# Recommender tower kernel: three or four one-hot chunks of each half stand ahead of the gram fills

## The reference, cut to what matters

```python
e = stack([tbl_t[ids[:, t]] for t in range(26)], axis=1)       # (2048, 26, 128)
combined = concatenate([dense[:, None, :], e], axis=1)          # (2048, 27, 128)
G = einsum('bfd,bgd->bfg', combined, combined)                  # one gram matrix for each sample
z = concatenate([dense, G[:, iu, ju], dense], axis=1)           # upper triangle, 607 columns
h = maximum(z @ W_top1 + b_top1, 0)                             # 512
h = maximum(h @ W_top2 + b_top2, 0)                             # 256
y = h @ W_top3                                                  # (2048, 1)
```

## Time and profile before

| | |
|---|---|
| median of 3 runs | 543.87 us |
| profiled execution | 548.43 us |
| its span | 546.6 us |
| TensorE busy | 418.0 us, 76% |
| VectorE busy | 275.6 us, 50% |
| GpSimd busy | 243.9 us, 45% |
| ScalarE busy | 142.9 us, 26% |
| mean granted TensorE clock | 0.881 of full speed |

### The profile page before, as it was taken

The page is one execution under the profiler, slowest core; times in us unless marked ns, Lnnn a source line. Parts: engine busy times, 40 slices in busy tenths (PEclk is TensorE's granted clock), DMA queues, the critical chain, the costliest instruction groups (busy, mean ns, idle before and its releaser), DMA issues.

```text
span 546.6 us, 10182 instructions
## 1 busy us (share of the span) xinstructions
PE 418.0 (76%) x4392; PEld 385.7 (71%) x4392; DVE 275.6 (50%) x365; ACT 142.9 (26%) x355; POOL 243.9 (45%) x264
## 2 busy tenths in 40 slices
PE   2477765759878596985969768794887949778998
PEld 2466664759776595975959768693886849767987
DVE  4389853854445454444454545445552465434322
ACT  4355121522122111222112222122221222112432
POOL 6726373553626355262553616446163552616100
PEclk9869995978889798787988879799787989979999
DMA  7954631221212112121221211222020311211000
GB/s 201 259 141 105 200 85 33 83 62 38 66 42 79 49 49 69 40 74 44 54 62 50 72 36 58 58 65 71 27 86 28 83 43 38 80 31 38 22 11 1
DMA packets 19775, 37.38 MB, mean 68 GB/s; under 512 B 5930, under 2 KB 8626, under 8 KB 19732
## 3 DMA queue, kind: packets, MB, share of 16 engines
q0 software_dynamic: 8192, 16.79, 11.5%
q1 hardware_dynamic: 5492, 9.85, 6.8%
q10 hardware_dynamic: 6048, 10.10, 6.0%
HBM read 36.71 MB, written 0.01 MB: 67 GB/s over the span
## 4 chain that ended last, share of the span: by engine, by line
PE 56%; another core or an unknown queue 19%; issue 10%; ACT 7%; DVE 5%; DMA 2%; SPq 1%; DVEq 0%; ACTq 0%
PE psB L431 19%; PE psG L457 14%; PE psB L506 7%; PE psB L415 6%; PE psB L513 6%; PE psB L500 3%; DVE one_hot L730 3%; ACT ET L633 2%; DMA ET<-tbl 2%; ACT ET L653 2%; PE psB L468 1%; DVE tab_lo L741 1%; ACT Zp L672 1%; ACT psG L605 1%
## 5 line engine op out<-in xcount | busy, mean ns | idle before, releaser
L354 POOL DMA_INDIRECT E<-tbl,gidx x256 | 243.0, 949 | 264.2 <-PE psB L415 163.5
L730 DVE TENSOR_TENSOR one_hot<-oidx,psR 125x1024 fp32r<-125x1024 int32 (+1 forms) x176 | 200.8, 1169 | 172.0 <-remote 130.7
L431 PE MATMUL psB<-one_hot,tab_hi 125*128 125x256 f32 x672 | 126.1, 308 | 24.4 <-issue 11.7
L457 PE MATMUL psG<-ET 128*52 128x52 f32 x2048 | 87.5, 259 | 70.8 <-issue 38.7
L457 PEld LDWEIGHTS psG<-ET 128*52 128x52 f32 x2048 | 79.2, 172 | 79.5 <-issue 45.6
L431 PE MATMUL psB<-one_hot,tab_lo 125*128 125x256 f32 x672 | 118.7, 296 | 14.4 <-issue 11.3
L431 PEld LDWEIGHTS psB<-one_hot,tab_hi 125*128 125x128 f32 x672 | 99.4, 202 | 31.7 <-issue 26.5
L431 PEld LDWEIGHTS psB<-one_hot,tab_lo 125*128 125x128 f32 x672 | 99.0, 201 | 16.7 <-issue 12.7
L633 ACT COPY ET<-psB 128x512 f32<-128x512 f32 x64 | 40.8, 638 | 89.2 <-PE psB L415 58.1
L777 DVE COPY_PREDICATED S<-second,psG 116x208 f32<-116x208 int32 x64 | 25.0, 391 | 50.1 <-ACT S L662 49.6
L662 ACT COPY S<-psG 116x208 f32<-116x208 f32 x64 | 21.3, 332 | 100.8 <-PE psG L457 95.3
(11 more groups left out here) (55 smaller groups left out, 217.3 us busy)
## 6 DMA issues: line engine op xcount, KB each, us to landing
oidx<-hot_idx ACTq DMA_DIRECT2D x35, 256.0 KB
E<-tbl,gidx POOLq DMA_INDIRECT x256
ET<-tbl SPq DMA_DIRECT2D x3, 448.0 KB
oidx<-hot_idx SPq DMA_DIRECT2D x5, 256.0 KB
dense<-dense_pairs SPq DMA_DIRECT2D x8, 128.0 KB
ZH<-tbl SPq DMA_DIRECT2D x2, 448.0 KB
S<-tbl SPq DMA_DIRECT2D x2, 448.0 KB
Zd<-dense_rows ACTq DMA_DIRECT2D x7, 128.0 KB, 2.0
```

The costliest lines, as they stand in the source:

```text
L354: nc.gpsimd.indirect_dma_start(E[:, n % SLOTS, i, :], None, gathered[feature_and_tile(n, i)[0]], bass.IndirectOffsetOnAxis(ap=gidx[:, 4 * ...
L431: product = nc.tensor.matmul(bank[:, t % 2 * DUO:(t % 2 + 1) * DUO], tab[0:ROWS_P, TABLE_BASE[t] + k0 + i, :], one_hot[0:ROWS_P, m % RING, ...
L457: gram = nc.tensor.matmul(psG[g % 2][q * LANE:q * LANE + M, a * M:(a + 1) * M], two[:, 0:M], two[:, PAIR:], start=True, stop=True)
L730: nc.vector.tensor_tensor(one_hot[0:ROWS_P, m % RING, 0:many], ids, rows, ALU.is_equal).then_inc(hot_full[m % RING], 1)
```

## The change

In every half that has chunks, the first of them go ahead of the gram fills: chunks 0, 1 and 2 in odd halves (`FILL_LAST[0]` is 3), chunks 11 to 14 in even ones. The rest are spread as before, among fewer steps. In half 2 the W1 steps belong to chunks 11 to 15, so four of the five go ahead of the gram fills with their chunks.

```diff
-        left = hots
+
+        ahead = FILL_LAST[0] if late else 4
+        first, left = hots[:ahead], hots[ahead:]
         if late:
             after = spread(left, parts(d - 1)[:M1]) if d else left
...
-        return grams + spread(turns, with_W1(after) if h == 2 else after)
+        if h == 2:
+            first, after = with_W1(first), with_W1(after)
+        return first + grams + spread(turns, after)
```

## The result

The changed kernel took 549.12 us (547.72 to 550.45, 4 runs) against 543.83 us beside it: ratio 1.0103, 95% interval 1.0079 to 1.0128. It is slower by 1.0%; the forecast was 533.4 us, faster by 1.9%. Its profiled execution took 550.45 us, with a span of 548.6. The profiled execution of the kernel before has a span of 546.6 and took 4.6 us more than that kernel's median, the changed kernel's only 1.3 more, so the two traces differ by 2.0 us where the medians differ by 5.3. Ratios here are taken over undisturbed executions alone, so they can differ a little from the quotient of two medians.

The account below looks back on a forecast made before the run. TensorE's completions, held back beside GpSimd's gathers, were taken as the bound. Even halves gaining 2.3 us and odd ones losing 0.8, times 7, gave 10.5 us off the 543.87 us median: 533.4 us, range 518 to 560.

Parts of the forecast that it names:

- C: Rival: even halves keep two runs of eight gathers, VectorE's builds delay gram copies; 22 us slower, 566; chance 0.18.
- D: Rival: even halves run sixteen gathers in one stretch; 24 us slower, 568, or 556 in one pair of two; chance 0.18.
- Point 4: Even halves' gathers: twelve plus four, release 17.1 us after the first gather instead of 23.4; 2.3 us gained.
- Points 1 and 2: Odd halves: moved chunks fill TensorE's idle, 2.9 to 1.0 us gained; builds ahead of VectorE's gram copy, 1.7 us lost.
- Point 5: Odd halves' gathers: two runs of eight remain, next first gather at 33.8 us against 33.0; 0.8 us lost.
- points 2 and 3: Builds ahead of VectorE's gram copy in odd halves, 1.7 us lost; even halves' early chunks and queue, 0.5 us lost.

Follow-up runs that it names:

- f1_change: The changed kernel itself, unaltered, measured again beside the kernel before (548.49 us): 549.15 us, ratio 0.9988.
- f2_from2: The change from half 2 on, half 1 keeping the order of the kernel before: 545.03 us, ratio 0.9933 to the kernel before.
- f4_from3: The change from half 3 on, halves 1 and 2 keeping the order of before, measured again: 546.73 us, ratio 0.9975 to the kernel before.
- e6_mid: The change in halves 3 to 13 only, VectorE's queue as in the change: 546.26 us, ratio 0.9948 to the kernel before.
- e4_queue: The whole change, but VectorE walks each half's four gram copies before the moved chunks' builds: 542.19 us, ratio 0.9963 to the kernel before.
- e5_mid_queue: The change in halves 3 to 13 only, with VectorE's gram copies ahead of the moved builds: 532.74 us, ratio 0.9806 to the kernel before.
- e1_odd: The change in odd halves only, even halves keeping the order of the kernel before: 552.43 us, ratio 1.0184 to the kernel before.
- e12_from3_queue: The change from half 3 on, including half 14, with VectorE's gram copies ahead of the moved builds: 536.17 us, ratio 0.9749 to the kernel before.
- e3_from3: The change from half 3 on, halves 1 and 2 keeping the order of before, first measurement: 545.91 us, ratio 1.0057 to the kernel before.

## Why the prediction was wrong

**Right.** What bounds the kernel: completions of TensorE held back beside GpSimd's gathers. The runs made that firmer than the trace could (549.7 to 401.6 us). The measured 549.1 us lies in the stated range of 518 to 560 only by the partial forms of C and D, not by the forecast. Point 4: even halves went to twelve and four gathers, release 17.0 us after the first (said: 17.1), next first gather 31.7 us after it (said: 32.0). Points 1 and 2: gram fills at 256.6, 22.3 us after the first gather (said: 20.6), with a wait of 1.46 us for VectorE (said: 1.7 in odd halves).

**Point 5 was wrong in its mechanism.** It kept two runs of eight in odd halves; they became twelve and four as well, and the distance is 32.4 us, not 33.8. The third transpose was let out early enough, or just after the eighth gather (`f1_change` shows eight, a pause of 1.3 us, four and four, at a distance of 32.1).

**The base of the sum was one pair.** I took 34.3 + 33.0 = 67.3 us for a pair; five pairs in a row average 66.0. The change's 64.3 is below my 65.8, so the two errors cancelled, by luck: 1.7 gained a pair in the two traces, 1.5 said. By kind of half, over halves 4 to 13, even ones went from 33.7 to 31.7 us (2.0 gained, 2.3 said), odd ones from 32.3 to 32.7 (0.3 lost, 0.8 said). The gain of the middle is in every trace of a kernel that moves these halves together, and it is lost at their borders:

| trace | halves moved | start to half 4 | half 4 to 14 | half 14 to end |
|---|---|---|---|---|
| before | none | 162.3 | 330.0 | 54.3 |
| after | 1 to 14 | 170.4 | 321.7 | 56.5 |
| f1_change | 1 to 14 | 170.1 | 320.3 | 57.0 |
| f2_from2 | 2 to 14 | 166.0 | 320.5 | 57.2 |
| f4_from3 | 3 to 14 | 168.4 | 320.7 | 57.2 |
| e6_mid | 3 to 13 | 165.9 | 321.4 | 54.2 |
| e4_queue | 1 to 14, queue turned | 170.1 | 314.8 | 56.0 |
| e5_mid_queue | 3 to 13, queue turned | 161.8 | 313.5 | 54.0 |

The last three columns are us between first gathers (the last one to the end of the span). The kernel before has one trace only, of an execution 4.6 us above its median, so the gain against it is an upper figure: `e6_mid` as a whole gained 2.9 us by the ratio, and `f2_from2` 3.7.

**The step that failed** is "the head, half 15 and the tail hold no moved chunk". Halves 1 and 2 do. I counted them as two of the fourteen gaining halves and used half 1 as the witness for twelve and four, with its transposes already 2.4 us apart. The change puts them at 0, 2.4, 3.8 and 6.1, and rival D's one long stretch happened exactly there. Moving half 1 costs 3.7 and 4.1 us in two pairs of runs, each within one set (3.7 and 3.0 by the ratios); in the first trace half 4 begins 8.1 us late. The stretch costs where half 2's chunks stand behind it (36.8 us to half 2) and not where half 2 keeps its order (30.4 in `e1_odd`); why is read from the traces only: fills at the lower granted clock and VectorE's builds and weight splits ahead of its copies. Of what I said of half 2 the weight copies alone turned out to cost nothing. The forecast had 1.5 us for each of seven pairs, 10.5 in all, and no term for any border. Half 14 was counted as a gain too, and in the trace it is a loss of 2.2.

**Rival C was half right.** Not in its eights and not in its 22 us, but in its cause: VectorE's queue costs 7 us over the kernel, where 1.7 in each of seven odd halves alone would be 12. My sum had it inside points 2 and 3 and took it off a gain that was too large.

**One reading of the kernel was wrong.** I wrote that no moved chunk ends a fill. Chunk 11 does, so in even halves ScalarE's copy of that fill and an index load also went ahead of the gram copies. In the middle it cost nothing that shows: in half 6 ScalarE copies the fill at 221.62 and is idle before the first gram copy at 225.92. In half 2 ScalarE's weight copies follow it, and its first gram copy comes at 97.92.

**What stays open.** The kernel before takes 543.8 to 549.7 us by the set, the change 549.1 both times. So the change's loss is 1.0% beside one measurement of the kernel before and nothing beside another. It is not simply the chip: the first and the fourth set are both on record as chip 8, with 544.3 and 548.5 us, while the change from half 3 on moved by 0.8 only (545.9 and 546.7). The traces show that something in the timing differs: the same changed kernel pauses 0.45 us after the eighth gather of half 3 in its first trace and 1.3 us in the fourth set's. The kernel before has no trace from the later sets, so the cause stays open. Why `e5_mid_queue` and `e12_from3_queue` beat the sum of their parts was not tried either; their traces hold a part of it: with VectorE's queue turned, half 3 begins 30.6 and 30.9 us after an unmoved half 2, where without it this border took 34.5, 34.6 and 33.3 (`e3_from3`, `f4_from3`, `e6_mid`). They are 1.9% and 2.5% faster than the kernel before.

## What to carry to other kernels

When a step is moved ahead on one queue, it moves ahead on every queue that walks the same list: look for the short instruction it now stands before, here a 0.39 us copy behind three builds of 1.22. Count a gain per repetition only over the repetitions that are alike, and work the first and the last ones out by themselves. And take the base of such a sum from many repetitions of the trace, not from the pair one happens to read.

## What the runs showed of the hardware

I had not expected how much GpSimd's indirect DMAs cost TensorE. Of the kernel's 544 to 550 us, 141 (544.3 - 403.3) to 148 (549.7 - 401.6) go when the 256 gathers of 128 rows from GpSimd go; as many bytes loaded by SyncE with plain loads cost nothing that shows (401.6 us, against 403.3 with 20 gathers only). Whether it is the issuing engine, the indirect form or the scattered rows was not tried. In a run of gathers (as from 228.93 to the release at 252.37 in the kernel before) completions flow for about 4 us, then come a few at a time, until some 2 us after the last gather; in half 1 a pause of 1.2 us did not end such a stretch (`f1_change`), one of 2.7 us did (`f2_from2`). The granted clock from 150 to 350 us is 0.87 with the gathers and 1.00 without them.
